# Source buckets in pieces of 256 rows, four pieces a unit, and the adds to the nodes moved between DVE's dependent steps

## What is computed

```python
Wh = h @ W + b
row, col = (edge_index[0], edge_index[1])          # src, dst
sc = jax.nn.softplus(deg_coeff[0] * deg_v + deg_coeff[1])
Wr = Wh[row]
Wc = Wh[col]
dot = jnp.sum(Wr * Wc, axis=-1)
nr = jnp.sqrt(jnp.sum(Wr * Wr, axis=-1))
nc = jnp.sqrt(jnp.sum(Wc * Wc, axis=-1))
sim = dot / jnp.maximum(nr * nc, EPS)
sim_pos = jax.nn.relu(sim)
sim_neg = -jax.nn.relu(-sim)
base = adj_v * sc * no_diag
prop_pos = jax.ops.segment_sum((base * sim_pos)[:, None] * Wc, row, num_segments=n_nodes)
prop_neg = jax.ops.segment_sum((base * sim_neg)[:, None] * Wc, row, num_segments=n_nodes)
return scale * (coeff[0] * prop_pos + coeff[1] * prop_neg + coeff[2] * Wh)
```

## Time and profile before

| | |
|---|---|
| device time, median of 3 runs | 9338.5 us (9328.59 to 9359.22) |
| profiled execution, own time | 9360.56 us |
| its span, first to last instruction | 9358.7 us |
| TensorE's granted clock, mean | 0.770 |
| busy share PE, DVE, ACT, POOL | 60%, 50%, 33%, 54% |
| HBM read and written | 497.93 MB, 301.41 MB (85 GB/s) |

### The profile page before, as it was taken

One profiled execution on the slowest core, in us unless ns is written; L12 is line 12 of the kernel. 1 busy time (PEld: TensorE's weight loads), 2 busy tenths in 40 slices (PEclk: granted clock), 3 DMA queues, 4 the chain that ended last, 5 costly groups with the idle time before them and its releaser, 6 DMA issues. The chain is left out here.

```text
span 9358.7 us, 104647 instructions
## 1 busy us (share of the span) xinstructions
PE 5654.9 (60%) x23358; PEld 3511.4 (38%) x23359; DVE 4682.0 (50%) x10739; ACT 3131.0 (33%) x6007; POOL 5096.4 (54%) x5308
## 2 busy tenths in 40 slices
PE   0067877887850677777777713343334334399997
PEld 0033444343420333333333312222222222299997
DVE  2545555555542333433333344555544455477777
ACT  0023333333320333333333311111100101299997
POOL 5666666666656666666666566666666666500000
PEclk9978788788775777777777756666666666699998
DMA  8233333333421333333333311111111111122221
GB/s 333 78 93 111 110 107 109 108 107 108 112 74 49 86 103 105 107 104 102 101 106 104 97 28 57 55 53 55 54 53 53 53 53 56 47 60 59 60 60 52
DMA packets 566845, 800.68 MB, mean 86 GB/s; under 512 B 163210, under 2 KB 307466, under 8 KB 566506
## 3 DMA queue, kind: packets, MB, share of 16 engines
q1 hardware_dynamic: 371944, 482.15, 17.1%
q0 software_dynamic: 172640, 195.75, 9.4%
q10 hardware_dynamic: 22178, 121.99, 3.3%
HBM read 497.93 MB, written 301.41 MB: 85 GB/s over the span
## 5 line engine op out<-in xcount | busy, mean ns | idle before, releaser
L699 POOL DMA_INDIRECT rows_by_src_bucket<-arena,put_idx x1568 | 1528.9, 975 | 923.0 <-issue 484.2
L628 POOL DMA_INDIRECT G<-h_rows,src_idx x1568 | 1482.4, 945 | 831.1 <-issue 463.6
L628 POOL DMA_INDIRECT G<-in_x,src_idx x1470 | 1397.0, 950 | 822.8 <-issue 489.4
L731 PE MATMUL ps_two<-ident,inj 128*128 128x128 f32 x2352 | 454.7, 326 | 2209.2 <-DVE xd_t L1170 1011.5
L1170 DVE TENSOR_TENSOR_SCAN xd_t<-same,xd_t,ps_two 128x512 f32<-128x512 bf16 x588 | 749.1, 1274 | 1509.0 <-remote 1177.4
L749 PE MATMUL ps_gv<-attr,w_attr 65*128 65x512 f32 x1568 | 1099.8, 840 | 175.5 <-issue 91.3
L731 PEld LDWEIGHTS ps_two<-ident,inj 128*128 128x128 f32 x2352 | 318.8, 165 | 2354.0 <-issue 1106.8
L752 PE MATMUL ps_gv<-arena,w_src 128*128 128x512 f32 x1568 | 1034.8, 797 | 0.0
L933 ACT COPY arena<-ps_out 128x512 f32<-128x512 f32 x392 | 230.6, 588 | 1873.8 <-remote 1330.3
L981 ACT COPY arena<-ps_two 128x512 f32<-128x512 f32 x196 | 115.6, 590 | 2186.1 <-remote 1692.4
L755 PE MATMUL ps_gv<-xd_t,w_dst 128*128 128x512 f32 x1568 | 780.0, 620 | 9.4 <-issue 9.4
(11 more groups left out here) (235 smaller groups left out, 9633.4 us busy)
## 6 DMA issues: line engine op xcount, KB each, us to landing
inj<-first_edge_rows SPq DMA_DIRECT2D x588, 256.0 KB
running_sums<-arena SPq DMA_DIRECT2D x392, 256.0 KB
same<-same_dst SPq DMA_DIRECT2D x1176, 64.0 KB
rows_by_src_bucket<-zeros ACTq DMA_DIRECT2D x98, 703.5 KB
first_edge_rows<-zeros ACTq DMA_DIRECT2D x56, 896.0 KB
attr<-in_attr_t SPq DMA_DIRECT2D x392, 128.0 KB
G<-h_rows,src_idx POOLq DMA_INDIRECT x1568
rows_by_src_bucket<-arena,put_idx POOLq DMA_INDIRECT x1568
```

The lines of the kernel that those rows point to most:

```text
L628: pool.indirect_dma_start(out_, None, table_in, bass.IndirectOffsetOnAxis(ap=index, axis=0)).then_inc(s, 16)
L699: pool.indirect_dma_start(bucket_d, bass.IndirectOffsetOnAxis(ap=put_idx[:, buf, k:k + 1], axis=0), put[:, buf, k], None).then_inc(s_added ...
L731: mm = pe.transpose(turned(ps_inj, j), inj[:, buf, j * P:(j + 1) * P], ident[:])
```

## The change

- A bucket is padded to whole pieces of PART = 256 rows, and a unit has PARTS = 4 pieces. The units fall from 248 to 224 (28 trips). A unit still has 1024 rows in eight tiles.
- The piece table has 896 entries in place of 512, so `start_buckets` and the transposes behind it handle IDS = 7 columns in place of 4, DVE converts it in four instructions in place of two, and it lies in row 0 of `attr`.
- `add_unit` is gone. The four adds of unit b-2 stand inside `weigh(b)`, one behind each of its first four steps, and the home addresses are loaded at the start of every `weigh`. `s_hadd` of unit b-2 is so counted up ahead of `s_wm` of unit b. The adds of the last two units follow the loop.
- The multiplication with the weight and the sign factor are formed from the unscaled dot product, ahead of the wait for ACT's root; what is left behind the root is the reciprocal, one combined step and one product.
- `load_unit` moves four runs of 536 B a partition in place of two of 1072 B.

```diff
-UNIT = 2 * COLS
+PARTS = 4
+PART = 2 * P
+UNIT = PARTS * PART
 NU = 8
-UNITS = -(-(EP // COLS + NT) // (2 * NU)) * NU
+UNITS = -(-(EP // PART + NT) // (PARTS * NU)) * NU
+IDS = UNITS * PARTS // P
...
     def then(self, instruction):
-        self.k += 1
-        instruction.then_inc(self.sem, 1)
-        self.engine.wait_ge(self.sem, self.at + self.k)
+        self.need(self.put(instruction))
+
+    def put(self, instruction):
+        self.k += 1
+        instruction.then_inc(self.sem, 1)
+        return self.k
+
+    def need(self, k):
+        self.engine.wait_ge(self.sem, self.at + k)
...
-        bucket_units = bucket_d[0:BROWS].rearrange("(u a p j) f -> u p a (j f)", a=2, p=P, j=TILES)
+        bucket_units = bucket_d[0:BROWS].rearrange("(u q p j) f -> u p q (j f)", q=PARTS, p=P, j=2)
...
-                if buf % NB == 0:
+                if buf % 2 == 0:
...
-                        bucket_at[0:1, 0, ds(h * (2 * NU) + 2 * buf, 2 * NB)], engines=(mybir.EngineType.PE,),
+                        bucket_at[0:1, 0, ds(h * (PARTS * NU) + PARTS * buf, 2 * PARTS)], engines=(mybir.EngineType.PE,),
...
+                for k in range(SLOTS):
+                    mm = pe.matmul(summed[buf % 2][:, k // 2], onehot[:, buf % NB, k], w_msg[:, buf % 2, k],
+                                   start=k % 2 == 0, stop=k % 2 == 1)
...
-                for c in range(TILES):
-                    then(v.tensor_scalar(junk_, ends, half_id[:, c:c + 1], 0.0, ALU.is_le, ALU.add,
-                                         accum_out=half_bucket[:, c:c + 1]))
+                for c in range(IDS):
+                    then(v.tensor_scalar(junk_, ends, part_id[:, c:c + 1], 0.0, ALU.is_le, ALU.add,
+                                         accum_out=part_bucket[:, c:c + 1]))
...
+                behind = (h, buf - 2) if buf > 1 else (h - 1, buf + NU - 2)
+                adds = buf > 1 or not at_start(h)
+                if adds:
+                    homes = load_homes(*behind)
                 dve.wait_ge(s_wr, udone(h, buf))
                 dve.wait_ge(s_unit[buf], h * 16 + 16)
-                then(v.tensor_tensor(two_halves(dots[:, 0]), picked[:, :, :, D], now[:, :, :, NORM_AT], ALU.mult))
+                both = steps.put(v.tensor_tensor(two_halves(dots[:, 0]), picked[:, :, :, D], now[:, :, :, NORM_AT],
+                                                 ALU.mult))
+                if adds:
+                    dve.wait_ge(s_outs, udone(*behind))
+                    dve.wait_ge(s_hadd, udone(*behind, 1))
+                    added = steps.put(add_part(homes, buf, 0))
+                steps.need(both)
                 v.tensor_scalar(dots[:, 1], dots[:, 0], SIM_EPS * SIM_EPS, None, ALU.max).then_inc(s_n2, 1)
+                if adds:
+                    steps.need(added)
+                    added = steps.put(add_part(homes, buf, 1))
                 v.tensor_tensor(prod.rearrange("p (a j) f -> p a j f", a=2), picked[:, :, :, 0:D], now[:, :, :, 0:D],
                                 ALU.mult).then_inc(s_dotted, 1)
+                if adds:
+                    steps.need(added)
+                    added = steps.put(add_part(homes, buf, 2))
                 dve.wait_ge(s_dotted, udone(h, buf))
-                then(v.tensor_reduce(dots[:, 2], prod, AX.X, ALU.add))
+                dot = steps.put(v.tensor_reduce(dots[:, 2], prod, AX.X, ALU.add))
+                if adds:
+                    steps.need(added)
+                    add_part(homes, buf, 3).then_inc(s_hadd, 1)
+                steps.need(dot)
+                v.tensor_tensor(dots[:, 3], dots[:, 2], flat[:, :, WEIGHT_AT], ALU.mult)
+                signed = steps.put(v.tensor_scalar(dots[:, 4], dots[:, 2], 0.0, coef[:, 11:12], ALU.is_gt, ALU.mult))
                 dve.wait_ge(s_nn, udone(h, buf))
-                then(v.reciprocal(dots[:, 3], dots[:, 1]))
-                then(v.tensor_tensor(dots[:, 2], dots[:, 2], dots[:, 3], ALU.mult))
-                then(v.tensor_scalar(dots[:, 4], dots[:, 2], 0.0, coef[:, 11:12], ALU.max, ALU.mult))
-                then(v.scalar_tensor_tensor(dots[:, 5], dots[:, 2], coef[:, 9:10], dots[:, 4], ALU.mult, ALU.add))
-                then(v.tensor_tensor(dots[:, 6], dots[:, 5], flat[:, :, WEIGHT_AT], ALU.mult))
+                root = steps.put(v.reciprocal(dots[:, 7], dots[:, 1]))
+                steps.need(signed)
+                scaled = steps.put(v.scalar_tensor_tensor(dots[:, 5], dots[:, 4], coef[:, 9:10], dots[:, 3], ALU.add,
+                                                          ALU.mult))
+                steps.need(scaled)
+                then(v.tensor_tensor(dots[:, 6], dots[:, 5], dots[:, 7], ALU.mult))
                 dve.wait_ge(s_outs, udone(h, buf, 2))
                 v.tensor_tensor(w_msg[:, buf % 2], flat[:, :, 0:D], along(dots[:, 6], D), ALU.mult).then_inc(s_wm, 1)
...
+            def load_homes(h, buf):
...
+            def add_part(homes, buf, q):
+                home = H[:, ds(homes[q], D)]
+                return v.tensor_tensor(home, home, summed[buf % 2][:, q], ALU.add)
+
+            pipeline(dve, (weigh, 0), steps=steps, per=9 * NU, n=NU, trips=UTRIPS)
```

More of the change, by code:

```diff
@@ L70 @@
 assert GROUPS % NB == 0 and NT % (2 * CH) == 0 and SEARCH * SEARCH == EP and N > (P - 1) * NT
+assert IDS * P == UNITS * PARTS and IDS <= 2 * TILES
 assert CLEAR_ROWS * BCLEARS * P >= BROWS and PAD_HALF <= ZW and NU == 2 * NB
@@ L242, in gnn @@
         onehot = tile(NB, SLOTS, P)
-        rows = [t.rearrange("p (a c) -> p a c", a=2) for t in (
+        rows = [t.rearrange("p (q c) -> p q c", q=PARTS) for t in (
             *(whole[:].rearrange("p b c -> p (b c)")[:, k * 2 * TILES * RW:(k + 1) * 2 * TILES * RW]
@@ L591, in load_unit @@
                     sp.wait_ge(s_wm, udone(h, buf, NU))
-                load(rows[buf], bucket_units[ds(h * NU + buf, 1)].rearrange("u p a c -> p (u a) c"), s_unit[buf])
+                load(rows[buf], bucket_units[ds(h * NU + buf, 1)].rearrange("u p q c -> p (u q) c"), s_unit[buf])
             pipeline(sp, (load_unit, 0), n=NU, trips=UTRIPS)
@@ L1324, in _ @@
             for k, width in enumerate((D + 1, D)):
-                v.tensor_scalar(bucket_at[0:1, k], ps_out[0:1], float(width), None, ALU.mult).then_inc(s_halves, 1)
+                for c, table in enumerate((ps_out, ps_pos)):
+                    n = min(COLS, IDS * P - c * COLS)
+                    turn = v.tensor_scalar(bucket_at[0:1, k, c * COLS:c * COLS + n], table[0:1, 0:n], float(width), None,
+                                           ALU.mult)
+                turn.then_inc(s_parts, 1)
             v.tensor_copy(reached[:, 0], base.rearrange("p c t -> p (c t)")).then_inc(s_reached, 1)
@@ L1386, in weigh @@
+                steps.need(scaled)
+                then(v.tensor_tensor(dots[:, 6], dots[:, 5], dots[:, 7], ALU.mult))
                 dve.wait_ge(s_outs, udone(h, buf, 2))
                 v.tensor_tensor(w_msg[:, buf % 2], flat[:, :, 0:D], along(dots[:, 6], D), ALU.mult).then_inc(s_wm, 1)
-            summed = [t[:, 0:2 * D].rearrange("p (a f) -> p a f", a=2) for t in (ps_pos, ps_out)]
-            homes = []
-            def add_unit(h, buf):
-                if buf % 2 == 0:
-                    dve.wait_ge(s_halves, 2)
-                    homes[:] = nc.values_load_multi_w_load_instructions(
-                        bucket_at[0:1, 1, ds(h * (2 * NU) + 2 * buf, 4)], engines=(mybir.EngineType.DVE,), min_val=0,
-                        max_val=(NT - 1) * D,
-                        skip_runtime_bounds_check_because="a count of bucket ends, at most NT - 1")[1]
-                dve.wait_ge(s_outs, udone(h, buf))
-                for a in range(2):
-                    home = H[:, ds(homes[2 * (buf % 2) + a], D)]
-                    add = v.tensor_tensor(home, home, summed[buf % 2][:, a], ALU.add)
-                    if a == 0:
-                        then(add)
-                add.then_inc(s_hadd, 1)
-                dve.wait_ge(s_hadd, udone(h, buf))
@@ L1408, in _ @@
-            pipeline(dve, (weigh, 0), (add_unit, 2), steps=steps, per=8 * NU, n=NU, trips=UTRIPS)
+            summed = [t[:, 0:PARTS * D].rearrange("p (q f) -> p q f", q=PARTS) for t in (ps_pos, ps_out)]
+            def load_homes(h, buf):
+                if at_start(h) and buf == 0:
+                    dve.wait_ge(s_parts, 2)
+                return nc.values_load_multi_w_load_instructions(
+                    bucket_at[0:1, 1, ds(h * (PARTS * NU) + PARTS * buf, PARTS)], engines=(mybir.EngineType.DVE,),
+                    min_val=0, max_val=(NT - 1) * D,
+                    skip_runtime_bounds_check_because="a count of bucket ends, at most NT - 1")[1]
@@ new lines, in add_part @@
+            def add_part(homes, buf, q):
+                home = H[:, ds(homes[q], D)]
+                return v.tensor_tensor(home, home, summed[buf % 2][:, q], ALU.add)
+            pipeline(dve, (weigh, 0), steps=steps, per=9 * NU, n=NU, trips=UTRIPS)
+            steps.begin()
```

(8 more changed lines are left out.)

61 lines of the change are left out of this document (30 added, 31 removed).

## The result

| | before | changed |
|---|---|---|
| median us | 9338.1 (9328.6 to 9359.2, 4 runs) | 9197.0 (9189.3 to 9203.4, 4 runs) |
| ratio | 1 | 0.984, 95% interval 0.982 to 0.9859 |
| profiled execution: own time, span | 9360.56, 9358.7 | 9201.23, 9199.4 |

The change makes the kernel 1.6% faster. The forecast was 9192, so it was 5 us too low, less than the scatter of either kernel's runs.

The account below looks back on a forecast made before the run. The last stage was taken as bound by a two-unit ring of waits across ACT, DVE and PE. Fewer, shorter steps save 151.4 us, additions cost 5: 9338.5 - 146 = 9192 us; range 9170 to 9236.

Parts of the forecast that it names:

- Units, -111: Last stage: 248 units become 224; the 24 fewer, at 4.62 us each, save 111 us.
- Step, 4.44: Last stage: ACT's turn of 4.43 us, plus stray waits, sets each step at 4.44 us; 223 steps take 990.1 us.
- The ring through the adds and root: Last stage before the change: dependencies across ACT, DVE and PE set the step, 9.28 us for two units, 4.64 each.
- X = 3.0: DVE's time in weigh from first step to messages, adds included: taken as 3.0 us, between 2.77 and 4.00.
- pick ring: Last stage: dependency from PE's pick through DVE's messages and PE's sum to the next pick, 4.23 us a unit.
- DVE by itself: Last stage: DVE's own series per unit, from one first step to the next, 4.0 us.
- What is added, 5 us: Extra setup between the parts and extra adds behind the loop: 5 us together.
- Loads: load_unit in the last stage: 512 runs of 536 B take at most 2.0 us of a step and cost nothing.
- Rival 1: DVE's weigh instructions each take full duration, adds in series: 3.60 us to the messages, 9212 us total; chance 0.05.
- Rival 2: Adds' address work in weigh lengthens DVE's stretch: 4.00 us gives 9257 us, near 3.8 gives 9232; chance 0.18.
- Rival 3: Last stage: DVE becomes the bound at 5.30 us a unit and the kernel slower, 9384 us; chance 0.03.
- Rival 4: DVE's new order in the last stage frees nothing: step stays 4.62 us, 9232 us; chance counted within Rival 2.

Follow-up runs that it names:

- e1: Changed kernel's 256-row pieces and 224 units, but DVE's old scaling and four adds in series behind the messages: 9436.6 us, ratio 1.0092 to the kernel before.
- e6: Changed kernel with seven instead of eight ACT activations a unit in make_marks: 7956.0 us in one run.
- e3: Changed kernel with adds between the steps but the old scaling, all behind the root: 9222.5 us, ratio 0.9866 to the kernel before.
- e4: Kernel before, with its 512-row pieces and 248 units, but DVE in the new order: 9299.4 us, ratio 0.9943 to the kernel before.
- e2: Changed kernel with new scaling, but the four adds in series behind the messages: 9266.0 us, ratio 0.9907 to the kernel before.
- e9: Changed kernel with 128-row pieces, eight a unit, 216 units, eight DVE adds a unit: 8199.9 us, ratio 1.01 to the kernel before.
- e7: Changed kernel with seven instead of eight PE transposes a unit in turn_marks: 8800.9 us in one run.
- e12: The kernel of e7 run again, four times: 8801.0, 8801.8, 8802.6 and 7985.2 us.

## Why the prediction was right, and where its terms were off

9192 were forecast and 9197 measured, and the mechanism is the one forecast: the units fell by 24, the adds came off the path, and ACT's own turn sets the step. Term by term:

- *Units, -111.* 224 units, every step at the old price would be 1030.6 in place of 1141.5. Right as a term of the sum; the old price was not to be had with the old order (e1, 4.97 inside a trip).
- *Step, 4.44.* It measured 4.456, 993.7 us for 990.1. The 3.6 us are in the main ACT's turn of its own loop, once in eight units 0.19 long, which I had not priced: 28 x 0.19 = 5.3, less the 0.01 a step (2.2) that I had put in for stray waits. The first trip adds 0.8: it takes 36.4 us against 35.66, while the clock is still rising. That ACT's turn is what binds was argued in the prediction and is shown by e6, where it goes away together with ACT's tile.
- *The ring through the adds and root.* That this ring, and no engine, set 4.62 rests on the kernel before: on its three waits above, and on DVE's own series there, 2.90 (as in e1, which has the same steps) + 0.61 + 0.57 for the two adds + 0.19 (as in e1) = 4.27, which is under PE's 4.41. e3 and e4 bear it out: with the adds out of the ring and little else changed, the step falls to 4.40. e1 and e2 do not test it. They measured 4.97 and 4.62 where the ring gave 4.99 and 4.64, but there DVE's own series has the same length and is what closes; that the numbers met is chance.
- *X = 3.0.* Measured 2.92, from a base of about 2.55 to 2.57 (2.60 predicted) and 0.35 to 0.37 for the adds (0.40 predicted). The pick ring is then (5.45 + 2.92)/2 = 4.19, under ACT's 4.43, and it didn't matter that X was 0.08 too high.
- *DVE by itself.* The 0.27 ahead of the next first step was partly a wait for PE, as its row says; without it the distance is 0.19. The rest of the 0.14 and 0.13 by which e1 and e2 were forecast too long lies in X, 2.90 for 2.96 and 2.55 for 2.60. In e1 and e2, where the adds stand behind the messages, this term is what binds; in the changed kernel DVE is ahead of PE, and the rival that hung on it (chance 0.03) did not come true.
- *What is added, 5 us.* Not seen. The stretch behind the last pick is 0.5 shorter; that in front of the first is moved by 11 us by POOL's scatter, so a setup of a few us can't be read in it. The term was within the scatter either way. Part of the good sum is luck: 3.6 too little in the step and 5 too much here nearly cancel, and the sum of -146 stands between the -148 of the traces' stage and the -141 of the medians.
- *Loads.* The share is 23.3% and the transfers land in 2.8 us; see below. No wait of L1011 for a load. Right. Of the signs of being wrong one shows once: PE's sum waits for the messages (L1428) for 1.6 us, one time in the window.
- *Register loads.* The homes are loaded once a unit, 224 times for 0.343 us, and DVE's row ahead of L1396 is a wait for PE, not for issue. Hidden, as said.
- *ACT over 98% busy.* 97.7%. There is 0.1 a unit between its instructions that no row counts as work. POOL's last scatter, said to stay within 10 us of 8142, was at 8130.5.
- *Rivals.* Rival 1 (adds in series, X = 3.60) is refuted by the rows above: L1442 starts 0.60 behind L1407, which runs 0.68. The sentence of the Trainium skill, "VectorE: DVE Perf Modes", "The DRAIN you can't avoid", that went with it is not what this kernel does. The same section goes on that an operation that isn't held starts earlier, and refers to "Two Vector instructions with no wait between them"; that is what the rows show, and the prediction had weighed the first alone. (The advice to minimize the number of operations stands on the same page of the Trainium skill under "Rules for kernel authors".) Rival 2 (X of 4.00) would need 1.4 for the adds, and they cost 0.35. It was also priced by the wrong bound: at X = 4.00 the prediction's own sum for DVE by itself, 4.00 + 0.69 + 0.27 = 4.96, is longer than its pick ring of 4.73, so the price was some 9308 and not 9257. Rival 3 would have DVE full; it is at 78%. Rival 4 is refuted by e4 and e3: the step fell to 4.40 inside a trip. Its price, the old 4.62, forgot the two more adds: e1, in which the order is the old one, has 4.97.
- *Sign and weight before the root.* I had let the whole gain of the new order come out of the rings together. Once the adds stand between the steps, this part is worth some 6 us (e3); with the adds behind the messages it is worth 0.35 a step (e1 to e2). The place of the adds is worth some 60 (e2 is 83 faster than before, the changed kernel 141 to 144), part of it the three falls of the clock in e2.
- *The clock.* The prediction took 1.00 in the stage as given. It held for the changed kernel and would not have for the kernels between it and before (e1, e2): an error of a size that none of the rivals had.

## What to carry to other kernels

When three engines are each 80 to 98% busy and the step is longer than the turn of any of them, look for a ring of waits across them that spans two or more units, add it up from one timeline, and take out of it whatever the next link does not need: here two adds, then the step fell to the turn of the slowest engine, ACT. Add up each engine's own series as well, and look which of its waits another engine ends: two sums of the same length can't be told apart by the time alone. Less work per pass (24 units fewer) and a shorter ring had to come together; the padding alone put two more adds behind the messages and lost 87 us. Before a loop body is unrolled further, count its instructions on every engine, and look for an instruction queue in the DMA view behind it.

## What the runs showed of the hardware

- **TensorE's clock can fall after short gaps, and a full load does not always bring it back.** In e1 it fell to 0.50 behind 23 of 27 waits of 1.00 us at the turn of the loops, and was back 3 to 14 us later; in e2 behind 3 of 26 waits of 0.64 us; in e9 after 4 us of near idleness. In e7 and in the profile of e12 it stayed at 0.50 for the whole last stage, in e7 with PE busy 300.00 of 300 us; two more of e12's four executions took the same time. The other kernels' profiles all reach 1.00 5 to 15 us behind the first pick. A wait of 1 us a trip cost e1 85 us by way of the clock.
- **A load's time on the DMA engines went nearly by its bytes at runs of 536 B, and rose by a quarter at 268 B.** A packet on q1 took 61 ns at 1072 B, 33 ns at 536 B (0.233 x 16 x 800 / 90816) and 20 ns at 268 B in e9 (0.224 x 16 x 950 / 171600). A unit's load, by the units loaded in each window (200, 172 and 165), took 16.7, 17.3 and 20.6 us of one engine's time. The share of e9 is no higher only because its steps are longer. The prediction had left it open between one price a packet and one a byte.
- **The part ahead of the last stage differed by 1220 us from chip to chip.** The kernel before took 9338 and 9349 us in the first two comparisons and 8116 and 8117 in the two behind them, on other chips; the picks of the changed kernel are 4.456 and 4.457 apart on either kind, so the difference lies ahead of the last stage. The one kind of indirect DMA whose landing both traces of the changed kernel show (99 loads by `block_idx`) took 9.8 us in the median on the first kind of chip and 3.2 us on the second, while the loads of the last stage took 2.8 and 2.9. That indirect DMAs are what differs fits this and wasn't tested.
